# Moving one routing's second rows to GpSimd and its coefficients six steps forward in a fused MoE and attention kernel

## The reference

```python
x = x + 0.5 * ffn(layernorm(x), gate_w, expert_bias, w1, w2, w3)
x = x + attn(layernorm(x), Wq, Wk, Wv, Wo)
x = x + 0.5 * ffn(layernorm(x), gate_w, expert_bias, w1, w2, w3)
```

## Time and profile before

| what | value |
|---|---|
| median of three runs | 738.44 us |
| lowest and highest | 736.34 and 741.41 us |
| the profiled execution's own time | 737.8 us |
| its span | 736.0 us |
| mean granted TensorE clock | 0.953 |
| busy share: TensorE, VectorE, ScalarE, GpSimd | 84%, 61%, 53%, 41% |

### The profile page before, as it was taken

The page is one execution under the profiler, slowest core; times in us unless marked ns, Lnnn a source line. Parts: engine busy times, 40 slices in busy tenths (PEclk is TensorE's granted clock), DMA queues, the critical chain, the costliest instruction groups (busy, mean ns, idle before and its releaser), DMA issues.

```text
span 736.0 us, 14989 instructions
## 1 busy us (share of the span) xinstructions
PE 621.3 (84%) x5080; PEld 475.7 (65%) x5080; DVE 446.4 (61%) x1164; ACT 390.6 (53%) x912; POOL 303.1 (41%) x312
## 2 busy tenths in 40 slices
PE   6399999999979778899899998899999999999100
PEld 6388999988857434455554554456989899999100
DVE  6955733235456989899999999973676322233211
ACT  1625764444422577778777787783457544444000
POOL 6067714565433373044000010005566077776474
PEclk9999999999999899999999999989999999999655
DMA  8358978787982454435334443016678878887322
GB/s 263 100 165 222 252 225 237 224 239 207 286 231 81 153 147 148 125 117 166 110 116 139 125 130 103 3 58 198 179 211 249 228 218 245 246 250 208 100 78 64
DMA packets 116586, 126.02 MB, mean 171 GB/s; under 512 B 12512, under 2 KB 99168, under 8 KB 116384
## 3 DMA queue, kind: packets, MB, share of 16 engines
q1 hardware_dynamic: 98544, 101.20, 45.7%
q0 software_dynamic: 9088, 18.63, 10.2%
q10 hardware_dynamic: 8880, 5.25, 2.3%
HBM read 89.37 MB, written 35.39 MB: 170 GB/s over the span
## 4 chain that ended last, share of the span: by engine, by line
PE 53%; DVE 24%; issue 6%; DMA 6%; POOL 5%; ACT 4%; SPq 1%; POOLq 0%; ACTq 0%; DVEq 0%
PE banks L684 13%; DVE mx L816 10%; PE banks L656 9%; PE banks L672 8%; PE banks L665 8%; POOL rows L588 4%; PE banks L1128 4%; PE banks L646 2%; PE banks L471 2%; ACT PT L1143 2%; DMA WR<-in_experts 2%; PE banks L1012 2%; PE banks L1101 1%; DVE resid L803 1%; DVE split L809 1%
## 5 line engine op out<-in xcount | busy, mean ns | idle before, releaser
L568 POOL DMA_INDIRECT xe<-routed_rows,idx x156 | 151.6, 972 | 224.7 <-PE banks L646 85.7
L816 DVE TENSOR_REDUCE mx<-banks 128x2 f32<-128x512 f32 x256 | 163.4, 683 | 8.9 <-PE banks L1103 7.7
L1143 ACT ACTIVATE PT<-banks 128x512 f32<-128x512 f32 x256 | 140.5, 604 | 36.4 <-PE banks L1114 34.1
L588 POOL DMA_INDIRECT rows<-slots_out,slot x128 | 124.0, 969 | 72.2 <-issue 27.8
L737 DVE TENSOR_TENSOR hidT<-banks,act 96x256 f32<-96x256 f32 (+1 forms) x92 | 34.9, 380 | 188.2 <-ACT act L718 187.9
L684 PE MATMUL banks<-WR,hidT 128*128 128x128 f32 x936 | 119.8, 275 | 0.6 <-ACT ye L727 0.6
L684 PEld LDWEIGHTS banks<-WR,hidT 128*128 128x128 f32 x936 | 111.9, 191 | 2.9 <-issue 1.0
L656 PE MATMUL banks<-xeT,WR 128*128 128x256 f32 (+1 forms) x368 | 86.1, 356 | 8.0 <-issue 3.8
L672 PE MATMUL banks<-xeT,WR 128*128 128x256 f32 (+1 forms) x368 | 82.8, 347 | 0.0
L665 PE MATMUL banks<-xeT,WR 128*96 128x256 f32 (+1 forms) x368 | 82.5, 347 | 0.0
L1128 PE MATMUL banks<-PT,V 128*32 128x256 f32 x1024 | 73.4, 407 | 4.5 <-ACT oT L1190 3.8
(11 more groups left out here) (160 smaller groups left out, 894.9 us busy)
## 6 DMA issues: line engine op xcount, KB each, us to landing
WR<-in_experts SPq DMA_DIRECT2D x92, 544.0 KB
stacks<-split SPq DMA_DIRECT2D x32, 384.0 KB
slots_out<-ye SPq DMA_DIRECT2D x156, 64.0 KB
QS<-stacks SPq DMA_DIRECT2D x64, 112.0 KB
KS<-stacks SPq DMA_DIRECT2D x64, 112.0 KB
routed_rows<-xn ACTq DMA_DIRECT2D x16, 256.0 KB, 5.3
routed_rows<-xn SPq DMA_DIRECT2D x12, 256.0 KB, 2.3
xe<-routed_rows,idx POOLq DMA_INDIRECT x156, 4.4
```

The source lines that it names most:

```text
L568: eng.indirect_dma_start(xe[:, i % XR, a, :], None, routed_rows[h], bass.IndirectOffsetOnAxis(ap=idx[h][:, tile:tile + 1], axis=0))\
L588: eng.indirect_dma_start(rows[:, k, t, :], None, slots_out[h], bass.IndirectOffsetOnAxis(ap=slot[h][:, k, t:t + 1], axis=0))\
L816: eng.tensor_reduce(mx[:, :, e, pair], maxima_bank(f)[:, :].rearrange("p (q n) -> p q n", q=2), AX.X, ALU.max).then_inc(s_max, 1)
L1143: eng.activation(PT[:, u % 4, 1 - k].rearrange("p t n -> p (t n)"), PS[f % 3], ACT.Exp, scale=scale).then_inc(s_exp2, 1)
```

## The change

VectorE no longer makes the second rows. `rows_gpsimd` is the old `rows_vector` without its yields, called by GpSimd behind its root for this half and ahead of the gathers: it waits for factor and offset and issues the 16 `tensor_scalar` instructions in one go. SyncE's order of the eight stores puts second rows earlier.

On VectorE pieces 11 to 22 follow step 98 and no longer 104; pieces 23 to 30 follow steps 100 to 107, one each; 31 and 32 follow step 108, 33 step 109, and 34 with its empty pieces step 110 (before: 23 at 106 to 30 at 114, 31 to 33 at 115, 34 at 116). Steps 111 to 115 carry nothing. Pieces 47 to 62 follow steps 116 to 122 (before 118 to 125).

On ScalarE the Exp follows step 99 and no longer 105. The 16 first rows follow steps 111 to 118 one by one and steps 119 to 122 in pairs (before: in pairs at steps 117 to 124).

On TensorE the counts follow step 115 and no longer 117, and the inverse step 126 and no longer 125.

```diff
-        def rows_vector(eng):
+        def rows_gpsimd(eng):
             eng.wait_ge(s_coef, 2 * 3)
             eng.wait_ge(s_comb, GC * HALVES)
             for t in range(TH):
                 eng.tensor_scalar(rows[:, 1, t, :], X[:, t, :], factor[:, 1, t:t + 1], offset[:, 1, t:t + 1],
                                   ALU.mult, ALU.add).then_inc(s_xv, 1)
-                if t % 4 == 3:
-                    yield
...
-            for k, c in ((0, 0), (0, 1), (0, 2), (1, 0), (0, 3), (1, 1), (1, 2), (1, 3)):
+            for k, c in ((1, 0), (0, 0), (1, 1), (1, 2), (0, 1), (1, 3), (0, 2), (0, 3)):
...
             root_gpsimd(pool, 8, 0)
+            rows_gpsimd(pool)
...
-            attention_scalar(act, side, spans((105, 105, 17), (117, 117, 23), (118, 124, 2), (125, 125, 1)))
+            attention_scalar(act, side, spans((99, 99, 17), (110, 110, 21), (111, 118, 1), (119, 122, 2), (123, 123, 1)))
...
-            attention_tensor(pe, side, spans((117, 117, 39), (125, 125, 35)))
+            attention_tensor(pe, side, spans((115, 115, 39), (126, 126, 35)))
...
-            side, made = chained(route_norm(dve, 8, 0, 1), route_vector(dve, 2, 0)), rows_vector(dve)
+            side = chained(route_norm(dve, 8, 0, 1), route_vector(dve, 2, 0))
...
-                             (made, spans((124, 124, 1), (125, 125, 2), (126, 126, 1)), None),
-                             (side, spans((72, 73, 1), (80, 81, 1), (88, 89, 1), (96, 96, 3), (97, 97, 1), (104, 104, 12),
-                                     (106, 107, 1), (109, 109, 1), (111, 113, 1), (114, 114, 2), (115, 115, 3),
-                                     (116, 116, 13), (118, 119, 2), (120, 121, 3), (122, 123, 2), (125, 125, 2)), PAIRS * (BATCH - 1) + 6))
+                             (side, spans((72, 73, 1), (80, 81, 1), (88, 89, 1), (96, 96, 3), (97, 97, 1),
+                                          (98, 98, 12), (100, 107, 1), (108, 108, 2), (109, 109, 1), (110, 110, 13),
+                                          (116, 117, 2), (118, 119, 3), (120, 122, 2)), PAIRS * (BATCH - 1) + 6))
```

## The result

The changed kernel took 741.48 us (median of 16 runs, 737.08 to 747.25) against 735.80 us for the kernel before in as many (731.21 to 741.41). The ratio is 1.007, with a 95% interval of 1.0044 to 1.0096, that is 3.2 to 7.1 us. A second set of runs gave 1.0069 (1.0036 to 1.0102). The profiled execution took 740.61 us with a span of 738.8, 2.8 us over the one before.

A forecast was written before the change was run, and what follows sets the result against it. VectorE, ScalarE and TensorE were taken to set the pace in turn through attention's end. Terms: +4.2 - 0.3 - 0.9 - 0.4 - 0.1 = +2.5 us, profiled 740.3, predicted median 740.9, range 735.5 to 746.

The forecast's parts named there:

- Part 1: Up to step 111: nine VectorE pieces moved ahead of its maxima make it 4.2 us later (3.0 to 5.6).
- rival a: Attention's end: the new order closes TensorE's idle gaps, the half-clock stretch stays away, up to 3.0 us back, 737.9; chance 0.18.
- Part 2: Steps 111 to 114: VectorE loses pieces 26 to 28, ScalarE gets four rows and sets the pace; gain 0.3 us.
- Part 3: Steps 115 to 119: pieces 31 to 34 no longer keep VectorE from step 116's division; gain 0.9 us.
- Part 4: Steps 120 to 124: four rows leave ScalarE at 123 and 124, but TensorE is busy; gain 0.4 us.
- Part 5: Step 125's exponentials to the first turn, inverse behind step 126: 13.9 us against 14.0, gain 0.1 us.
- Part 6: Edits costed at nothing, among them GpSimd's rows: 0.6 us each, 10 us in all, up to 2.2 a row hidden.
- Rival (b): Hand-over: VectorE's pieces fit into unseen slack, 738.2, or 735.3 if the gather's 2.9 us count in full; chance 0.20.
- (d): GpSimd's row costs over 2.2 us; at 3 us each, 16 rows end 13 us late, 754; chance 0.04.
- rival (c): Steps 110 to 115: GpSimd's rows hold VectorE up, 12 x 0.3 = 3.6 us, 744.5; chance 0.11.
- the 1 us of the estimate: By the shared-SBUF rule, GpSimd's rows hold up pieces 33 and 34 once or twice: 742 instead of 741.

The follow-up runs named there:

- choices-early: Kernel before with pieces 11 to 30 and ScalarE's Exp at the new steps, pieces 31 to 34 at the old 115 and 116; ratio to before 1.0049.
- pieces-late: early-inverse with pieces 26 to 33 in pairs at steps 114 to 117, 34 at 118, ScalarE's rows one step later, counts behind 118; ratio to before 1.0058.
- pieces-early: Kernel before with only VectorE's pieces and ScalarE's Exp at the new steps; ratio to before 1.0081.
- early-inverse: Kernel before with second rows on GpSimd, pieces 32 to 34 behind step 116's division, inverse behind step 124, no 16 filling matmuls; ratio to before 0.9985.
- rows-on-GpSimd: Kernel before with only the second rows on GpSimd and SyncE's new order of stores; ratio to before 1.0012.

## Why the prediction was right in sign and range, and where its terms failed

I forecast +2.5 us and 740.9, in a range of 735.5 to 746; the median was 741.48 and the difference 5.7 us of medians, 3.2 to 7.1 by the interval. That the time came within 0.6 us is luck: my base was the median of three runs, 738.44, and sixteen gave 735.80, so the loss is over twice my forecast. The direction and its cause hold: VectorE's pieces, moved ahead of the last maxima, cost more than everything that the change frees. The profiled pair gave +2.8.

Part 1 forecast 4.2 us at step 111 and the profile has 4.19, but not by the mechanism that I gave. Only 1.60 us are there at step 108, and step 109 adds 2.4: the choices-early trace, which has the same instructions up to the fall and then full clock, adds 0.89 there, so about 1.5 us are the half clock. That leaves 2.7 us at step 111 for pieces worth 5.55: VectorE took up more than the 0.97 us I allowed, some of the cost came only behind step 111, and the half clock, which I had left out, made up for it. So 4.2 was hit by luck. The step that failed is "The sum is 5.55 us. VectorE's idle time takes some of it up: 0.51 us at 451.05 and 0.46 at 458.02". Pieces at steps 111 to 114 had been nearly free, as pieces-late shows, but similar ones cost in front of step 110: choices-early moved 2.9 us of work there and paid 2.27. I took the hiding capacity from gaps of VectorE in the timeline. It was larger in some steps (0.08 us of shift for three pieces at steps 100 to 102) and not to be read there. What I left out is that the idleness which this makes on TensorE may bring the half clock; I had it only as a loss that could go away (rival a), not as one that could come at this place.

Part 2 forecast a gain of 0.3 from step 111 to 115 and the profile has a loss of 5.73 - 4.19 = 1.54. Pieces-early, without ScalarE's rows there, loses 0.98: its shift grows by 1.22 us up to step 113, where that of choices-early, without pieces 31 to 34, stays at 2.27. VectorE does pieces 33 and 34 at 465.52 and 467.38 us there, on either side of the start of step 111 (466.79), so part of what part 1 prices arrives only here. The rest, 0.56, is the four rows of ScalarE and what GpSimd's rows beside VectorE cost (at most 0.23, below); no run parts them. ScalarE was busy for 6.80 of the 8.61 us, 79%, where I had said over 95%: it was not the pace there. I had expected VectorE's pieces, gone from here, to leave time, but pieces-late shows that there was 0.23 us to be had, and choices-early has 0.24.

Part 3 forecast a gain of 0.9 and got 5.73 - 4.89 = 0.84, but only about half by the cause named. The division at step 116 no longer waits behind pieces 31 to 34, yet TensorE still stood for it:

```profile
480.65 0.63 PE L1010 MATMUL banks<-CT,oT 128*128 128x128 f32 x4 [0.44 <-DVE on L1233]
```

The wait shrank from 0.87 us to 0.44, as it did in choices-early and early-inverse, whose step 118 came 0.43 and 0.44 us sooner against step 117. The other 0.4 us is about one row of ScalarE (two took 0.77): behind step 117 the changed kernel makes one and not two. That part no run shows alone.

Part 4 forecast 0.4 and got 4.89 - 3.35 = 1.54. From 120 to 122 the shift is flat at 4.89, as said; then the half clock, of which before had 6.0 us and more, was shorter: the window of steps 120 to 124 stands at 0.84 against 0.73 and 0.72. That is rival (a) in part.

Part 5 forecast 13.9 us from step 125 to the turn and got 13.87 (the gain is 3.35 - 3.20 = 0.15), with the half clock behind the inverse that I had priced at 1.5 (the product with V took 1.94 us).

Part 6 held. GpSimd's row took 0.45 us on average where I had 0.6 from memsets and a power; the first gather waited for the indices, and the turn came at 510.34 against 510.5. Rival (b) fell with pieces-early and rows-on-GpSimd, (d) with the 7.0 us.

Of rival (c), rows held by sharing with GpSimd, a trace of truth is there. VectorE's instructions by line, 466 to 487 us, of the changed kernel:

```profile
L814 DVE TENSOR_REDUCE mx<-banks 128x2 f32<-128x512 f32 x12 | 7.6, 684 | 0.1
L351 DVE TENSOR_TENSOR_SCAN upto<-CT,taken 128x128 f32<-128x128 f32 x1 | 0.6, 572 | 0.0
L353 DVE TENSOR_TENSOR place<-upto,taken 128x128 f32<-128x128 f32 x1 | 0.4, 360 | 0.0
```

The same in pieces-early, where GpSimd was idle:

```profile
L816 DVE TENSOR_REDUCE mx<-banks 128x2 f32<-128x512 f32 x10 | 6.3, 683 | 0.1
L351 DVE TENSOR_TENSOR_SCAN upto<-CT,taken 128x128 f32<-128x128 f32 x1 | 0.4, 412 | 0.0
L353 DVE TENSOR_TENSOR place<-upto,taken 128x128 f32<-128x128 f32 x1 | 0.3, 292 | 0.0
```

Piece 34's two instructions, with two SBUF inputs each, ran beside GpSimd's rows and took 0.16 and 0.07 us longer; the maxima, which read PSUM, 0.001. The Trainium skill (GPSIMD Engine Reference, Key points) names just this contention, and the trace agrees; it is 0.23 us in all, not the 1 us of the estimate, because only two instructions met it. The second repeats in all eight traces where GpSimd's rows run at this place (0.36 us against 0.29 in the six others), the first only in the three of the changed kernel's order (0.57); in rows-on-GpSimd it took 0.42, beginning 0.3 us behind the first row.

What stays open is the rest between the traces, 3.2 us from step 92 to the turn and 0.4 behind it, and the 5.7 of the medians. It may be noise, since the interval begins at 3.2 us; but pieces-early and choices-early, too, lost more in their runs than in their traces at the turn. In 16 runs after, the mean granted clock was 0.9515, in 35 further runs before 0.9547; within these two sets the time falls by 0.5 to 0.7 us for 0.001 of it, so 0.0032 is 1.6 to 2.2 us. This would fit more half clock after than before, but pieces-early lost 0.8% at a clock of 0.9542, so it is not the whole of it. The first two profiles don't show it either. From step 92 to the turn, before and then after:

```profile
429.48:507.97 78.49, 69.72 (x721) 40.64 (x721) 63.15 (x176) 55.53 (x121) 3.81 (x4) 0.93 0.30 93
```

```profile
428.65:510.34 81.69, 70.77 (x720) 40.12 (x721) 59.45 (x160) 55.92 (x121) 10.91 (x20) 0.94 0.29 89
```

Either way about 10 us of the stretch are at half clock. What step 108 lost, steps 120 to 124 got back, so in this pair the clock hardly has a net part in the 3.2 us. Nor does a single execution's total say much: step 92, in front of which nothing was changed, started between 426.80 and 434.18 us in the fourteen traces.

That the half clock at step 108 is caused by TensorE's idleness rests on four traces of five against none of eight, and on the run with extra matmuls; the fifth had the same instructions up to there. With one execution to a trace it is likely, not shown.

## What to carry to other kernels

Work slipped between the steps of a pipeline is free or dear by the step, and the busy share of its engine doesn't tell which: VectorE, 97% busy, hid all but 0.23 of 1.92 us of pieces in one place, and some seven steps earlier 2.27 of 2.9 us of such work became loss. Take the piece out in a run before believing in its price. Work freed in a stretch where another engine is the pace comes back at most as the gap that it had made there, and here only half of it: a wait of 0.87 us shrank to 0.44. And a stretch made slower may cost a second time through TensorE's clock, here 1.5 us: price what a stretch at full clock could still lose, not only what one at half clock could win.

## What the runs showed of the hardware that I had not expected

TensorE's clock fell to half in the middle of attention. In the 8.02 us before, TensorE had been busy for 5.95, and its longest gap was 0.86 us, a wait for VectorE's maxima:

```profile
456.36 0.28 PE L1099 MATMUL banks<-KS,QS 56*128 56x256 bf16 x1 [0.86 <-DVE mx L814]
```

In four executions the clock fell just under 1 us later; in a fifth (choices early), with the same instructions from step 92 up to that point and starts within 0.03 us, it did not. The kernels differ at this place only by pieces that come after the fall. So these starts alone don't decide it, and what does is open. The fifth's granted clock before step 92 was 0.97 on average, the four's 0.98 or 0.99; no run shows whether that bears on it.

A `tensor_scalar` of 128x128 float32 with two scalars for each partition took GpSimd 0.45 us on average, 1.3 times VectorE's 0.34, with 16 issued in a row and nothing of it visible on the maxima beside it (684 against 683 ns).
